# Last stage of a conv-attention-MoE kernel: loop written out, projection and turned chunks issued in small pieces between the experts' units

## What is computed

```python
x = x + _L0_conv_ref(_gn(x), ...)                   # convolutions and a mixing by Gram matrices
t = _to_tokens(x)                                   # 3136 tokens of 32 channels per image
t = t + _L1_attn_ref(_ln_t(t), Wq, bq, Wk, bk, Wv, bv)
t = t + _L1_ffn_ref(_ln_t(t), router_w, router_b, expert_w, expert_b)
```

```python
router_probs = softmax(x @ router_w + router_b)
top_p, top_i = jax.lax.top_k(router_probs, 2)
top_p = top_p / jnp.sum(top_p, axis=-1, keepdims=True)
expert_out = jnp.einsum('bnd,edc->bnec', x, expert_w) + expert_b
gathered = jnp.take_along_axis(expert_out, top_i[..., None], axis=2)
return jnp.einsum('bnk,bnkc->bnc', top_p, gathered)
```

## Time and profile before

| | us |
|---|---|
| median of 3 runs (lowest to highest) | 2794.78 (2792.41 to 2795.09) |
| the profiled execution | 2795.67 |
| its span | 2793.9 |
| PE, DVE, ACT, POOL busy in it | 2439.7, 2368.1, 1600.3, 407.0 |
| the last stage, from its first projection to the end | 2288.9 to 2793.9 |

### The profile page before, as it was taken

One profiled execution on the slowest core, in us unless ns is written; L12 is line 12 of the kernel. 1 busy time (PEld: TensorE's weight loads), 2 busy tenths in 40 slices (PEclk: granted clock), 3 DMA queues, 4 the chain that ended last, 5 costly groups with the idle time before them and its releaser, 6 DMA issues. The chain is left out here.

```text
span 2793.9 us, 48267 instructions
## 1 busy us (share of the span) xinstructions
PE 2439.7 (87%) x18454; PEld 987.3 (35%) x18454; DVE 2368.1 (85%) x4218; ACT 1600.3 (57%) x2106; POOL 407.0 (15%) x456
## 2 busy tenths in 40 slices
PE   3888878379999999999999999999999987778776
PEld 1343333112222222222222222222222236666664
DVE  4577776589999999999999999999999927888887
ACT  1143343237777777777777777777777753233332
POOL 0021121300000000000000000000000003545545
PEclk9999999569999999999999999999999985666666
DMA  7687592410201222202202202202200012223221
GB/s 173 174 222 225 182 275 90 147 54 1 59 21 39 58 73 50 59 1 59 59 1 59 58 1 59 59 1 59 59 1 24 24 45 72 70 70 104 70 69 24
DMA packets 68108, 206.19 MB, mean 74 GB/s; under 512 B 20630, under 2 KB 33554, under 8 KB 61234
## 3 DMA queue, kind: packets, MB, share of 16 engines
q1 hardware_dynamic: 64034, 185.27, 23.9%
q0 software_dynamic: 3040, 15.57, 1.5%
q10 hardware_dynamic: 816, 2.46, 0.3%
HBM read 80.14 MB, written 61.31 MB: 51 GB/s over the span
## 5 line engine op out<-in xcount | busy, mean ns | idle before, releaser
L1299 DVE TENSOR_REDUCE at_XM<-at_psX 128x1 f32<-128x448 f32 x2688 | 1546.2, 619 | 90.6 <-PE at_psX L1150 69.8
L1216 ACT ACTIVATE at_PR<-at_psS 128x896 f32<-128x896 f32 x1344 | 1162.9, 915 | 454.5 <-PE at_psS L1126 452.5
L1168 PE MATMUL at_psV<-at_PR,at_V 128*32 128x448 f32 x5376 | 645.9, 552 | 0.1
L1126 PE MATMUL at_psS<-at_US,at_KS 128*128 128x448 f16 x2688 | 636.8, 357 | 0.6 <-ACT at_PR L1216 0.2
L1150 PE MATMUL at_psX<-at_KS,at_US 64*128 64x448 f16 x1344 | 490.3, 365 | 65.0 <-DVE at_XM L1299 43.0
L1150 PE MATMUL at_psX<-at_KS,at_UH 64*128 64x448 f16 x1344 | 490.3, 365 | 0.0
L1150 PEld LDWEIGHTS at_psX<-at_KS,at_US 64*128 64x128 f16 x1344 | 124.6, 93 | 721.3 <-DVE at_XM L1299 661.7
L1126 PEld LDWEIGHTS at_psS<-at_US,at_KS 128*128 128x128 f16 x2688 | 201.2, 98 | 273.8 <-ACT at_PR L1216 118.7
L1265 POOL CAST at_mrow<-at_mt 7x128 f16<-7x128 f32 x64 | 17.9, 279 | 1611.8 <-DVE at_mt L1318 1258.9
L1568 POOL TENSOR_TENSOR fi_WE<-fi_WE 128x256 f32<-128x256 f32 (+1 forms) x224 | 213.0, 979 | 172.6 <-DVE fi_WE L1622 171.6
L1622 DVE TENSOR_TENSOR fi_WE<-fi_psE,fi_WT 128x512 f32<-128x512 f32 (+1 forms) x208 | 132.8, 666 | 43.9 <-PE fi_psE L1471 34.1
(11 more groups left out here) (205 smaller groups left out, 2109.6 us busy)
## 6 DMA issues: line engine op xcount, KB each, us to landing
sums<-at_O SPq DMA_DIRECT2D x16, 1568.0 KB, 6.4
fi_SUMS<-sums SPq DMA_DIRECT2D x16, 1568.0 KB, 6.6
sb_stacks<-sb_T SPq DMA_DIRECT2D x64, 270.5 KB, 7.8
sb_stacks<-sb_Xp SPq DMA_DIRECT2D x64, 248.8 KB, 9.5
sb_stacks<-sb_Xp SPq DMA_DIRECT2D x64, 248.0 KB, 5.8
sb_stacks<-sb_T SPq DMA_DIRECT2D x64, 172.5 KB, 11.1
at_KS<-key_stacks SPq DMA_DIRECT2D x32, 208.0 KB, 6.8
fi_RES<-residual SPq DMA_DIRECT2D x16, 400.0 KB, 7.1
```

Source lines behind the costliest of these rows:

```text
L1126: last = nc.tensor.matmul(psS[:, at % 2, k, 0:TILE], KS[:, b, (2 * c + k) * P:(2 * c + k + 1) * P], US[:, b, t * TILE:(t + 1) * TILE], sta ...
L1168: last = nc.tensor.matmul(psV[C * q:C * q + C, 0:TILE], V[:, b, G * k + q, :], PR[:, (n * 2 * STEPS + 2 * q4 + q // 2) % PRS, q % 2, :], s ...
L1216: nc.scalar.activation(PR[:, f % PRS], psS[:, at % 2, :, 0:TILE], ACT.Exp).then_inc(p_ready, 1)
L1299: nc.vector.tensor_reduce(o, psX[:, (at + j) % 3, 0:TILE], AX.X, ALU.max).then_inc(x_done, 1)
```

## The change

`finish` is written out for all 17 steps, with constants in place of registers (`beyond(n, k)` becomes `n > k`). On TensorE the two halves of the projection are cut in two each and stand ahead of the experts' units 2, 3, 4 and 5; the turned chunks come in six pieces of 4 or 5 ahead of units 7 to 12; the router stands behind unit 12. On VectorE weigh 3 moves ahead of the variance, 5 ahead of the reciprocal, 6 ahead of the low half; the mean's own operation is folded into XH, one operation of the Newton step goes, and one of the gates (WT is now (SEL1 + e SEL2) / (1 + e)). ScalarE's, GpSimd's and SyncE's orders stay.

```diff
 def newton_rsqrt(link, eng, r, v, t):
     link(eng.tensor_tensor(t, r, r, ALU.mult))
-    link(eng.tensor_tensor(t, t, v, ALU.mult))
-    link(eng.tensor_scalar(t, t, -0.5, 1.5, ALU.mult, ALU.add))
-    return link(eng.tensor_tensor(r, r, t, ALU.mult))
+    link(eng.scalar_tensor_tensor(out=t, in0=t, scalar=-0.5, in1=v, op0=ALU.mult, op1=ALU.mult))
+    return link(eng.scalar_tensor_tensor(out=r, in0=t, scalar=1.5, in1=r, op0=ALU.add, op1=ALU.mult))
...
-        def steps(eng, step):
-
-            for n in range(FIRST):
-                step(n, n % TURN, n // 2)
-            with eng.Fori(0, (N - TURN) // TURN) as i:
-                for n in range(FIRST, FIRST + TURN):
-                    step(i * TURN + n, n % TURN, i * 2 + n // 2)
-            for n in range(N - 1, N + 1):
-                step(n, n % TURN, n // 2)
+        def steps(step):
+
+            for n in range(N + 1):
+                step(n, n % TURN, n // 2)
...
 # TensorE, step
-                if more:
-                    project(n + 1, mb, r + b, (0,))
-                if old:
-                    experts(m, mb, (2, 3, 4))
-                if more:
-                    project(n + 1, mb, r + b, (1,))
-                if old:
-                    experts(m, mb, (5, 6))
+                for i, u in enumerate((2, 3, 4, 5)):
+                    if more:
+                        h, w = i // 2, NP // 2
+                        project(n + 1, mb, r + b, h, range(w) if i % 2 == 0 else range(w, NP + h))
+                    if old:
+                        experts(m, mb, (u,))
+                if old:
+                    experts(m, mb, (6,))
                 if new:
                     pe.wait_ge(z16_ready, n + 1)
                     pe.wait_ge(z_high, n * 2 + 2)
-                for s in range(KSETS):
+                for i, u in enumerate(range(7, NU)):
                     if new:
-                        turn_tokens(n, s)
+                        turn_tokens(n, range(NC * i // (NU - 7), NC * (i + 1) // (NU - 7)))
                     if old:
-                        experts(m, mb, (s + 7,))
+                        experts(m, mb, (u,))
                 if new:
                     router(n, b)
-                if old:
-                    experts(m, mb, (11, 12))
...
 # VectorE, step
                 mark(nc.vector.tensor_reduce(lsum[:], T1[:, c], AX.X, ALU.add))
-                settled()
-                mark(nc.vector.tensor_scalar(lsum[:], lsum[:], 1.0 / C, None, ALU.mult))
                 weigh(m, mb, (1,))
                 settled()
-                nc.vector.tensor_tensor(XH[:], T1[:, c], per_token(lsum[:]), ALU.subtract).then_inc(t1_cen, 1)
-                weigh(m, mb, (2,))
+                nc.vector.scalar_tensor_tensor(out=XH[:], in0=per_token(lsum[:]), scalar=-1.0 / C, in1=T1[:, c],
+                                               op0=ALU.mult, op1=ALU.add).then_inc(t1_cen, 1)
+                weigh(m, mb, (2, 3))
...
-                weigh(m, mb, (3, 4))
+                weigh(m, mb, (4, 5))
                 dve.wait_ge(t1_std, n + 1)
...
                 nc.vector.memset(XH[:, :, 0:1], 1.0).then_inc(xh_ready, 1)
-
+                weigh(m, mb, (6,))
+
+                dve.wait_ge(xh_ready, n + 1)
                 dve.wait_ge(z_high, n * 2 + 1)
...
-                weigh(m, mb, range(5, NU))
+                weigh(m, mb, range(7, NU))
...
-                link(nc.vector.tensor_scalar(g1[:], g2[:], 1.0, None, ALU.add))
-                link(nc.vector.reciprocal(g1[:], g1[:]))
-                mark(nc.vector.tensor_tensor(g2[:], g2[:], g1[:], ALU.mult))
-                mark(nc.vector.tensor_tensor(SEL1[:], SEL1[:], per_token(g1[:], E), ALU.mult))
+                mark(nc.vector.tensor_scalar(g1[:], g2[:], 1.0, None, ALU.add))
                 settled()
-                link(nc.vector.tensor_tensor(SEL2[:], SEL2[:], per_token(g2[:], E), ALU.mult))
-                link(nc.vector.tensor_tensor(WT[:, b], SEL1[:], SEL2[:], ALU.add))
+                mark(nc.vector.tensor_tensor(SEL2[:], SEL2[:], per_token(g2[:], E), ALU.mult))
+                mark(nc.vector.reciprocal(g1[:], g1[:]))
+                settled()
+                link(nc.vector.tensor_tensor(SEL1[:], SEL1[:], SEL2[:], ALU.add))
+                link(nc.vector.tensor_tensor(WT[:, b], SEL1[:], per_token(g1[:], E), ALU.mult))
```

More of the change, by code:

```diff
@@ L42 @@
 GR = 2 * XW
[L44 to L45 removed]
+ORDER_0, ORDER = 14, 46
 class Ahead(NamedTuple):
@@ L1422, in step @@
                 b = c % 2
-                if beyond(n, 0) and (not isinstance(n, int) or n + 1 < N):
+                if n > 0 and n + 1 < N:
                     load(n + 1, 1 - b)
-                if beyond(n, 1):
+                if n > 1:
                     store(n - 2, b)
-            steps(sp, step)
+            steps(step)
             store(N - 1, 1)
@@ L1434, in _, with project, turn_tokens @@
         def _(pe):
[L1435 to L1445, removed]
-                    last.then_inc(o_full, 1)
[L1448 to L1451, removed]
+            def project(n, b, r, h, part):
+                if h == 0 and part[0] == 0:
+                    pe.wait_ge(sums_in[b], (r + 1) * 16)
+                if n > 0 and part[0] == 0:
+                    pe.wait_ge(o_done, n * 2 + h - 1)
+                for q in part:
+                    a = (h * NP + q) * P
+                    last = nc.tensor.matmul(psO[:, h, q * (C + 1):(q + 1) * (C + 1)], SUMS[:, b, a:a + P],
+                                            wv[:], start=True, stop=True)
+                if part[-1] == NP + h - 1:
+                    last.then_inc(o_full, 1)
+            def turn_tokens(n, chunks):
+                for k in chunks:
+                    s, q = divmod(k, 8)
+                    if q == 0 and (n > 0 or s >= 2):
+                        pe.wait_ge(zs_ready, n * KSETS + s - 1)
                     last = nc.tensor.transpose(psK[:, s % 2, q * P:(q + 1) * P],
-                                               Z16[:, 8 * s + q].rearrange("p s c -> p (s c)"), ident16[:])
-                last.then_inc(k_full, 1)
+                                               Z16[:, k].rearrange("p s c -> p (s c)"), ident16[:])
+                    if q == 7 or k == NC - 1:
+                        last.then_inc(k_full, 1)
             def router(n, b):
                 pe.wait_ge(zs_ready, n * KSETS + KSETS)
-                if beyond(n, 1):
+                if n > 1:
                     pe.wait_ge(out_ready, n - 1)
@@ L1478, in sums @@
                     pe.wait_ge(folded, n * QSETS + s + 1)
-                    if s == 0 and beyond(n, 0):
+                    if s == 0 and n > 0:
                         pe.wait_ge(out_ready, n)
-                    if s == 4 and (not isinstance(n, int) or n + 1 < N):
+                    if s == 4 and n + 1 < N:
                         pe.wait_ge(lg_ready, n + 2)
@@ L1492, in step @@
                 m, mb, mc = n - 1, 1 - b, (c - 1) % TURN
-                old = beyond(n, 0)
-                new = not isinstance(n, int) or n < N
-                more = not isinstance(n, int) or n + 1 < N
-                if more:
-                    project(n + 1, mb, r + b, (0,))
-                if old:
-                    experts(m, mb, (2, 3, 4))
-                if more:
-                    project(n + 1, mb, r + b, (1,))
-                if old:
-                    experts(m, mb, (5, 6))
+                old = n > 0
+                new = n < N
+                more = n + 1 < N
+                for i, u in enumerate((2, 3, 4, 5)):
[4 more added lines that the diff above has]
+                        experts(m, mb, (u,))
+                if old:
+                    experts(m, mb, (6,))
                 if new:
@@ L1521, in _ @@
             pe.wait_ge(fin.w_ready, 1)
-            project(0, 0, 0, (0, 1))
-            steps(pe, step)
+            for h in range(2):
+                project(0, 0, 0, h, range(NP + h))
+            steps(step)
         @block.scalar
@@ L1536, in step @@
                 b = c % 2
-                if not isinstance(n, int) or n < N:
+                if n < N:
                     act.wait_ge(t1_cen, n + 1)
@@ L1560, in step @@
                     nc.scalar.activation(g2[:], gap[:], ACT.Exp).then_inc(gap_exp, 1)
-            steps(act, step)
+            steps(step)
             to_image(N - 1, 1, (N - 1) // 2)
@@ L1586, in step @@
                             fold(s - 1, E // 4).then_inc(folded, 1)
-                if not isinstance(n, int) or n + 1 < N:
+                if n + 1 < N:
                     residual(n + 1, (c + 1) % TURN, r + b)
             residual(0, 0, 0)
-            steps(pool, step)
+            steps(step)
         @block.vector
@@ L1602, in settled @@
             def settled():
-                dve.wait_ge(order, base[0] + done[0])
+                dve.wait_ge(order, done[0])
             def link(ins):
@@ L1641, in step @@
                 b = c % 2
```

(7 more changed lines are left out.)

31 lines of the change are left out of this document (12 added, 19 removed).

## The result

The changed kernel takes 2838.3 us (median of 4 runs, 2834.8 to 2843.6) against 2793.6 for the kernel before: ratio 1.0155, interval 1.0141 to 1.0169, so 1.6% slower. The forecast was 2840. The profiled execution took 2843.55 us.

The account below looks back on a forecast made before the run. VectorE and TensorE, about equally busy, bound the last stage's 14 steps through waits on each other, plus loop cost. Profiled 2795.67 + 46.8 (steps of 33.4) - 2 (first stage) = 2840.5, less 0.9: 2840 us; own range 2822 to 2860, widened 2805 to 2862.

Parts of the forecast that it names:

- Projection in pieces: TensorE, last stage: 38 projection matmuls at 0.208 us delay unit 5's weighing to 10.59, reciprocal to 11.19 instead of 6.53.
- Newton's step: VectorE, last stage: first two operations still held by GpSimd's fold, only the third saved; XH at 13.60 us.
- Turned chunks and router: Last stage: first chunk at 17.15 instead of 12.11 us; LG's first reduction 7.4 behind, less 0.3, at 24.2.
- Gates: VectorE, LG's reduction to next step: 0.7 off for folds, 0.2 for small operations; tail 9.2 instead of 10.08 us.
- The ambiguous term: Gates, SEL2's product against GpSimd's residual: 0.5 us gained if ahead of it, otherwise 0.1 lost; 0.2 gained assumed.
- The loop: Last stage, 14 steps: writing out the loop worth up to 10.2 us, already in the summed new step.
- the 0.3 taken off for the clock: Turned chunks: 0.3 us off a step, since such unbroken stretches ran partly at the high clock before.
- First stage: Newton's step, called 20 times there, saves between 0 and 4.2 us; half assumed, 2 us off.
- B: Rival: TensorE's clock rises in some steps or late in the stretch; step 31, +13, 2807 us; chance 0.06.
- C: Rival: fetching written-out code stalls once a step, 3 us; +42, 2882 us; chance 0.04.
- A: Rival: TensorE's clock rises in the projection pieces; step 28.4, -23 over 14 steps, 2770 us; chance 0.10.

Follow-up runs that it names:

- Experiments 1: Changed kernel with TensorE's projection put back whole, VectorE's new order kept; 2837.7 us, ratio 1.0161 against the kernel before.
- experiments 2: Changed kernel with VectorE's weighing order put back, TensorE's projection pieces kept; 2776.5 us, ratio 0.9938 against the kernel before.
- experiment 3: Changed kernel with the projection pieces behind unit 2 cut to 6 matmuls in place of 38 for images 2 to 15; 2780.7 us, ratio 0.9955.
- Experiment 4: Changed kernel with 116 columns in place of 33 in each projection matmul, order and waits kept; 2798.1 us, ratio 1.0018 against the kernel before.
- 6: Changed kernel with both TensorE's whole projection and VectorE's weighing order put back; 2769.9 us, ratio 0.9900 against the kernel before.
- Experiment 9: Kernel of 8 with unit 3 weighed ahead of the variance and unit 4 alone ahead of the reciprocal; 2728.0 us, ratio 0.9760.
- experiment 7: Kernel of 6 with turned chunks in four sets and the router ahead of units 11 and 12 again; 2777.2 us, ratio 0.9930.
- 5: Kernel before with only its last stage's loop written out; 2780.1 us, ratio 0.9939 against the kernel before.
- 8: Kernel of 6 with VectorE's divisions for the next image moved ahead of the wait for LG; 2744.3 us, ratio 0.9817.
- 10: Kernel of 8 with 116 columns in place of 33 in each projection matmul; 2741.9 us, ratio 0.9807.

## Why the prediction was right, step by step

The times of the sum, from w0, against the changed kernel's step that starts at 2361.65:

| | forecast | measured |
|---|---|---|
| w3, w4, w5 | 4.34, 7.26, 10.59 | 4.22, 7.05, 10.30 |
| reciprocal | 11.19 | 10.91 |
| XH | 13.60 | 13.31 |
| first turned chunk | 17.15 | 16.93 |
| reduction of LG | 24.2 | 24.28 |
| next w0 | 33.4 | 33.65 |
| 14 steps, more than before | 46.8 | 46.3 |
| mean step | 33.4 | 33.36 |

*Projection in pieces.* The 38 matmuls at the low clock stood in front of e5 as said. Experiments 1 to 3 show that it is the pair that costs: projection at 1.2 GHz in front of e5, and e5's weighing in front of the reciprocal. With either the second or the matmuls taken away the loss is gone; with the pieces alone put back it is not. Experiment 4 adds that the low clock is most of the price of the matmuls: 40 us of the 57.6 in experiment 3. Against 6, the pieces cost 6.6 us (2776.5 less 2769.9; 7.35 by the 14 steps), VectorE's order on top of them 61.8 (2838.3 less 2776.5). Twelve matmuls and a unit took 2.82 us, not 2.92, which is why w3 to w5 come somewhat earlier than in the sum.

*Newton's step.* That w5 starts folds which hold the first two operations was right (1.13 and 0.65, end 2374.71, where GpSimd's folds end at 2374.66), and the scalar_tensor_tensor of 25 columns costs 0.19 as assumed. Experiment 9 moves that collision away, and fills the 0.34 us wait for the squares, together for 13.4 us in the 14 steps. One more collision I had not foreseen: w3 moved ahead makes the variance's tensor_scalar take 0.45.

*Turned chunks and router.* The sum gave 7.1 (7.4 less 0.3), which is also the mean of the 14 steps; the chain was 7.35 in this step (2378.58 to 2385.93) and 6.62 in the one that starts at 2462.59 (2479.52 to 2486.14), where the chunks' matmuls get shorter from 2482.5 on. Eight of the 14 steps are of the first length, 33.65, and six of the second, 32.98. What the pieces of chunks do as a part stands in two terms of the sum: L1678 up to 0.3 later, and 0.7 off the gates because the folds end sooner behind it. Experiments 6 and 7 measured 0.36 later and 0.81 off, so the two terms were about right, and together they are the 6.2 us gained. It was the expectation for experiment 7 that looked at L1678 alone and left the folds out.

*Gates.* The ambiguous term went the other way: SEL2's product reaches the residual after it has begun and takes 2.05 us, so the 0.2 gain was 0.1 lost (from L1678 to the next w0 it is 10.22 in 7 and 10.08 in 5). The folds end 1.9 us behind L1678, as said, and that gave 0.85 (10.22 less 9.37) where 0.7 was taken. The tail was 9.37, not 9.2.

*The loop.* Right in sign, short in size: 15 us, not 10.2. As the new step was summed by itself, the 10.2 didn't enter the total; the distances taken from that one long step did, and the 0.3 taken off for the clock about made up for them.

*First stage.* I took 2 us off. The profiles don't settle it: the last stage starts at 2290.50 in the changed kernel and at 2288.75 in the one before, between 2284.7 and 2288.3 in the nine kernels of the experiments that share its first stage, and at 2293.5 in that of 5, which has the old one. By the medians the change costs 44.7 us, 1.6 less than its steps. I leave this open: no run shows the 2 us. The sum for the profiled execution was 2840.5 and it took 2843.55. That the forecast meets the median within 2 us is closer than its terms deserve: the first stage and the gates were taken too short, the units too long, and these cancel in part.

*Rivals.* B and C are out: the clock is 0.50 between units 2 and 5 and the reciprocal comes 10.9 us after w0 in all 14 steps, and no step of the changed kernel has a stall for issue on VectorE. A's mechanism was shown in 4, by work that the changed kernel doesn't have. The Trainium skill ("TensorE: Matmul & The Clock Gate", the section on the clock gate) has the gate follow how busy the engine is; here the same order of instructions, occupied without a break either way, stayed at 0.50 with 33 columns and went to 1.00 with 116. Read as busy time in the profile, that sentence would have given the wrong sign. The trace of before had a longer row against that reading than the 5.3 us used in the prediction: the 21.10 us at 0.50 shown in experiment 4.

## What to carry to other kernels

Before moving an item of one engine ahead in another's order, write down what stands in front of it on the engine that makes it, at the clock that stretch is granted: here three calls moved by some microseconds cost 62 us, and the profile of before had both numbers. Work that "hides" beside other work hides only as long as nobody asks for what is queued behind it. And see which small operations of VectorE run beside GpSimd's: sometimes the cheapest gain is to move the one that starts GpSimd. Last, compare steps in which one wait differs: where the end of the step stays put all the same, as in experiments 2, 6 and 8 to 10, another engine sets it.

## What the runs showed of the hardware

- A float32 matmul with a 128x128 weight load takes the same here with 33 and with 116 columns: 0.22 us each at 1.2 GHz (2.61 and 2.63 for 12) and 0.12 at 2.4 GHz (2.87 for 24 in the earlier trace rows, 1.72 for 14 in experiment 4). With 33 columns the clock stayed at 0.50 through 21.10 us of unbroken work, with 116 it went to 1.00 in the same place; in the changed kernel that made 40 us less in the whole program.
- An operation of VectorE with two inputs in SBUF was held until GpSimd's instruction ended (2374.71 and 2374.66 in the changed kernel): 25 columns take 0.19 us alone, 1.13 beside a fold, 1.35 and 1.52 beside the residual; a tensor_scalar of 25 columns takes 0.18 and 0.45. The weighing, with one input in PSUM, takes 0.69 either way. The Trainium skill ("VectorE: DVE Perf Modes", the section on two Vector instructions with no wait between them) names a second read interface into SBUF that VectorE shares with GpSimd; the durations of the two-input operations agree with that.
- A loop over 3 rounds of 4 steps cost 15 us here by the medians, 14.0 by the 14 steps: 3.3 at each of the two ways back to its head, and the rest spread over the steps.
